# A graph message sum in blocks of 512 edges with one plain mask, made earlier and kept as bytes

## The reference, cut to what matters

```python
y = linear(layernorm(x)) * node_attr              # per node: 64 scalars y0, 64 vectors y1 of 3
w = silu(edge_scalars @ fc_w1) @ fc_w2            # per edge: 4 x 64 weights w0..w3
g0, g1 = y0[src], y1[src]                         # per edge, gathered
a = edge_attr[:, 1:4]                             # per edge: one vector of 3
scalars = [w0 * g0,  w2 * (g1 . a)]               # . is the sum over the 3 components
vectors = [w1 * g1,  (w3 * g0) * a]
agg = segment_sum([scalars, vectors], dst)        # per node: 8 x 64 numbers
```

## Time and profile before

| | us |
|---|---|
| median of 3 runs | 1990.52 (1987.57 to 1991.15) |
| the profiled execution | 1992.24 |
| its span, first instruction to last | 1990.5 |
| mean granted TensorE clock over the span | 0.938 of 2.4 GHz |
| busy: TensorE, VectorE, ScalarE, GpSimd | 1761.1, 1125.7, 1021.4, 1109.6 |

### The profile page before, as it was taken

How to read it: one execution, slowest core, us unless ns; L and a number is a source line. 1 busy time by engine, 2 the same in 40 slices (tenths; PEclk the granted TensorE clock), 3 DMA queues, 4 the chain that set the end, 5 groups by cost and what they waited for, 6 DMA issues and landing times. The chain is left out here.

```text
span 1990.5 us, 38467 instructions
## 1 busy us (share of the span) xinstructions
PE 1761.1 (88%) x9911; PEld 1434.7 (72%) x9911; DVE 1125.7 (57%) x2792; ACT 1021.4 (51%) x3052; POOL 1109.6 (56%) x1499
## 2 busy tenths in 40 slices
PE   2799999999899839999755999999999999995999
PEld 1466666666566729999634899888999887774887
DVE  6644333333411665544494999999999973233122
ACT  5455545555443612322246777777777745552221
POOL 6788888888600014555347888888888830000343
PEclk7899999999999559999977999999999999996999
DMA  8767777778640246667456777777777761564553
GB/s 235 221 214 248 246 238 242 242 238 266 210 153 0 65 103 213 208 212 217 148 126 204 210 218 215 215 214 218 216 213 218 209 172 52 172 188 116 177 176 120
DMA packets 229316, 376.43 MB, mean 189 GB/s; under 512 B 66200, under 2 KB 114427, under 8 KB 229117
## 3 DMA queue, kind: packets, MB, share of 16 engines
q1 hardware_dynamic: 174908, 222.13, 36.8%
q0 software_dynamic: 52224, 150.15, 25.2%
q10 hardware_dynamic: 1984, 1.79, 0.3%
HBM read 275.38 MB, written 99.57 MB: 188 GB/s over the span
## 5 line engine op out<-in xcount | busy, mean ns | idle before, releaser
L1963 POOL DMA_INDIRECT msg_got<-y_dram,block_src x416 | 417.9, 1004 | 101.7 <-issue 93.2
L441 POOL DMA_INDIRECT ffn_w<-xn_dram,block_src x384 | 364.4, 949 | 96.0 <-issue 87.5
L1984 ACT ACTIVATE msg_scaled<-msg_plain,msg_w 128x125 f32<-128x125 f32 x1044 | 312.0, 386 | 95.2 <-DVE msg_plain L2016 95.2
L556 PEld LDWEIGHTS sum_ps_bank<-ffn_w,sum_onehot 128*125 128x125 f32 x928 | 171.6, 193 | 191.1 <-issue 175.4
L556 PE MATMUL sum_ps_bank<-ffn_w,sum_onehot 128*125 x928 | 254.3, 399 | 50.0 <-DVE sum_onehot L898 26.1
L886 DVE TENSOR_TENSOR agg<-sum_ps_bank,agg 125x256 f32 x232 | 98.6, 425 | 282.9 <-PE sum_ps_bank L556 278.4
L655 ACT ACTIVATE sum_space<-sum_ps_bank,sum_rec 128x128 f32<-128x128 f32 x416 | 130.1, 364 | 202.1 <-PE sum_ps_bank L543 200.4
L543 PE MATMUL sum_ps_bank<-sum_fc,sum_space 128*128 128x512 f32 x416 | 211.5, 593 | 1.3 <-ACT sum_space L644 1.3
L2005 PEld LDWEIGHTS msg_ps_z<-msg_prod,msg_scaled 128*125 128x125 f32 x1416 | 174.5, 189 | 6.8
L2005 PE MATMUL msg_ps_z<-msg_prod,msg_scaled 128*125 128x128 f32 x1416 | 175.2, 274 | 0.0
L2045 DVE TENSOR_TENSOR agg<-msg_ps_z,agg 125x512 f32 x232 | 159.8, 689 | 22.0 <-DVE agg L2045 1.8
(11 more groups left out here) (346 smaller groups left out, 3252.5 us busy)
## 6 DMA issues: line engine op xcount, KB each, us to landing
edge_w<-sum_space SPq DMA_DIRECT2D x52, 1040.0 KB, 5.2
msg_w<-edge_w SPq DMA_DIRECT2D x174, 260.0 KB
ffn_run_w<-in_L_ffn_w SPq DMA_DIRECT2D x64, 512.0 KB
x_sb<-edge_w SPq DMA_DIRECT2D x58, 260.0 KB
ffn_rows<-agg SPq DMA_DIRECT2D x25, 448.0 KB
ffn_w<-in_L_ffn_w SPq DMA_DIRECT2D x16, 512.0 KB, 8.7
wd<-in_L_ffn_Wd SPq DMA_DIRECT2D x8, 1024.0 KB, 8.9
msg_got<-y_dram,block_src POOLq DMA_INDIRECT x416, 3.7
```

The source lines that it names most:

```text
L441: pool.indirect_dma_start(got[:, (b + 1) % RING, u, :], None, k.x if b < RAW else k.xn_dram, bass.IndirectOffsetOnAxis(ap=k.block_src[:, b ...
L556: last = pe.matmul(ps_sum[n % ZB][0:P, :], onehot[n % OB][:, u, :], got[:, ds(need % RING, 1), u, :].rearrange("p o d -> p (o d)"), start= ...
L1963: pool.indirect_dma_start(got[:, (b + 1) % RING, u, :, :].rearrange("p k v -> p (k v)"), None, k.y_dram, bass.IndirectOffsetOnAxis(ap=k.bl ...
L1984: last = act.activation(scaled[s % MB][:, x, c, :], plain[s % MB][:, c, :], ACT.Copy, scale=w[s % RS][:, c, D + x:D + x + 1])
```

## The change

The message stage goes over blocks of 512 edges instead of 256: NB4 = 104 blocks, NP4 = NB4 + T - 1 = 128 pairs, one step each, with four half blocks that all belong to the same pair.
- The three scaled masks are gone. One plain mask per half block sums all eight groups of 64 in a single product of 512 columns. What the scaled masks did is done on the values: VectorE forms g1 times a for the three components (`along`), adds them up, and multiplies by w2; ScalarE multiplies w3 * g0 (kept in a ninth slot of `prod`) by each component of a, twelve copies of 64 elements.
- The plain mask isn't compared in this stage. During the neighbour sum VectorE writes the masks of all 128 pairs as bytes, one instruction of 500 elements each (`mask_bytes`), spread over pairs 24 to 177. SyncE stores them to DRAM, four pairs at a time (256 KB). In the message stage SyncE loads them and ScalarE turns a pair's 500 bytes into floats.
- The tables for 512-edge pairs (`pair4_need`, `pair4_tile`, `pair4_dst`, `block4_done`) are made at the start of the neighbour sum, on VectorE and TensorE, ahead of the statistics of the gathered blocks. ScalarE's two copies of the edge attributes come after the third and fourth normalised group instead of the fourth and fifth.
- GpSimd's gathers stay 416 of the same size; its ring is 16 blocks of 512, and it looks for free room once in 16 blocks of 256, against a pair number that it loads from `block4_done`.

The diff, cut to its core:

```diff
@@ sum_neighbours
+    def bytes_due(n):
+        return min(NP4, max(0, (n - 24) * 5 // 6 + 1))
+    def bytes_from(j):
+        return j * 128 // 100
@@ SyncE
             for g in range(NW):
+                for j in range(NBY):
+                    if bytes_from(j) == g:
+                        sp.wait_ge(bytes_made, BY * (j + 1))
+                        sp.dma_start(k.bytes[j, :, :], held[j % HELD]).then_inc(bytes_stored[j % HELD], 16)
                 sp.wait_ge(w_kept, QB * (g + 1))
...
@@ TensorE
+            pe.wait_ge(four_ready, 5)
+            for h in range(2):
+                pe.matmul(ps_four[:, h:h + 1], ranks..., minus[:, h:h + 1], start=True, stop=(h == 0))
...
+            pe.wait_ge(past_made, 4)
+            pe.wait_ge(chosen_made, 4)
+            for h, (at, n) in enumerate(HALVES):
+                pe.matmul(ps_rows4[0:1, 0:NP4], even[0:n, :], past4[0:n, h, :], start=(h == 0), stop=(h == 1))
...
+            pe.wait_ge(shifted, 4)
+            pe.wait_ge(chosen_made, 6)
+            for c in range(CH):
+                for h, (at, n) in enumerate(HALVES):
+                    last = pe.matmul(ps_field4[:, c, :], dst_fb[h][0:n, :, c % KC], chosen_half[c // KC][0:n, h, :],
+                                     start=(h == 0), stop=(h == 1))
@@ ScalarE
-                if g == 3:
-                    act.wait_ge(tables_made, 1)
+                if g == 2:
+                    act.wait_ge(tables_made, 4)
@@ VectorE, between scales(4) and gathered_statistics(0)
+            dve.tensor_copy(ranks, k.tri[:, 0:128:2]...).then_inc(four_ready, 1)
+            dve.tensor_tensor(twins, ...)
...
+            dve.wait_ge(starts_ready, 2)
+            chain(dve.tensor_scalar(first4[:, :], ps_four[:, 0:2], -1.0, None, ALU.mult))
...
+            dve.wait_ge(rows_ready, 2)
+            chain(dve.tensor_tensor(tile4_row[0:1, :], ps_rows4[0:1, 128:128 + NP4], k.iota[0:1, 0:NP4], ALU.add))
...
+            dve.wait_ge(field_ready, 2)
+            dve.scalar_tensor_tensor(k.pair4_dst[:, :, :].rearrange("p n c -> p c n"), ...)
+            dve.wait_ge(tables_made, 4)
             gathered_statistics(0)
@@ VectorE, loop over the pairs
+            def mask_bytes(j):
+                if j % BY == 0 and j >= HELD * BY:
+                    dve.wait_ge(bytes_stored[j // BY % HELD], 16 * (j // (HELD * BY)))
+                dve.tensor_tensor(held[...], ps_lanes[:, :].unsqueeze(1).to_broadcast([128, CH, P]),
+                                  k.pair4_dst[:, j, :].unsqueeze(2).to_broadcast([128, CH, P]), ALU.is_equal).then_inc(bytes_made, 1)
                 if n >= 1:
                     add_sum(n - 1)
+                for j in range(bytes_due(n - 1), bytes_due(n)):
+                    mask_bytes(j)
@@ sum_messages, GpSimd
-                if b > AHEAD:
-                    pool.wait_ge(made, (b - AHEAD + 1) // 2)
+                if b >= 2 * RING4 and b % (2 * HOLD4) == 0:
+                    last = b // 2 - HOLD4 - 1
+                    done = pool.value_load(k.block4_done[0:1, last:last + 1], min_val=1, max_val=NP4)
+                    pool.wait_ge(made, done)
+                    pass_on(pool, freed)
@@ ScalarE
+            def mask(n):
...
+                act.activation(plain[n % MB]..., held[n // BY % YB][:, n % BY, :], ACT.Copy).then_inc(masked, 1)
+            def split(n):
+                act.wait_ge(opened, n + 1)
                 for c in range(CH):
                     for x in range(3):
-                        last = act.activation(scaled[s % MB][:, x, c, :], plain[s % MB][:, c, :], ACT.Copy, scale=...)
+                        last = act.activation(p[:, c, 5 + x, :], p[:, c, 8, :], ACT.Copy, scale=w[n % RS][:, c, D + x:D + x + 1])
@@ TensorE
+                for c in range(CH):
+                    last = pe.matmul(ps_z[n % ZB][0:P, :, :], plain[n % MB][:, c, :], prod[n % XB][:, c, 0:8, :],
+                                     start=(c == 0), stop=(c == CH - 1))
@@ VectorE
+            def open_products(n, need):
+                dve.tensor_tensor(p[:, :, 0:9:8, :], v[:, :, 0:4:3, :], y[:, :, 0:1, :].to_broadcast([128, CH, 2, MUL]), ALU.mult)
+                dve.tensor_tensor(t[:, :, :, :], y[:, :, 1:4, :], w[...][:, :, D:D + 3]..., ALU.mult).then_inc(along_made, 1)
+            def close_products(n, v, y):
+                dve.tensor_tensor(t[:, :, 0, :], t[:, :, 0, :], t[:, :, 1, :], ALU.add).then_inc(along_made, 1)
+                dve.tensor_tensor(p[:, :, 1:4, :], v[:, :, 1:2, :].to_broadcast([128, CH, 3, MUL]), y[:, :, 1:4, :], ALU.mult)
+                dve.wait_ge(along_made, 3 * n + 2)
+                dve.tensor_tensor(t[:, :, 0, :], t[:, :, 0, :], t[:, :, 2, :], ALU.add).then_inc(along_made, 1)
+                dve.wait_ge(along_made, 3 * n + 3)
+                dve.tensor_tensor(p[:, :, 4, :], v[:, :, 2, :], t[:, :, 0, :], ALU.mult).then_inc(made, 1)
```

289 lines of the change are left out of this document (172 added, 117 removed).

## The result

The changed kernel took 2046.81 us in the median (2043.9 to 2057.02), the kernel before 1990.0 beside it: ratio 1.0296, 95% interval 1.0257 to 1.0335. I had put 2003.5 and the range at 1990 to 2040: the sign was right, the size far too small.

What follows compares the result with a forecast made beforehand. GpSimd's gathers (544 us) were taken to bound the message stage, VectorE (531) close behind. Adding 12 us at the neighbour sum's start and 1 at the message stage gave 2005 profiled, 2003.5 as a median; range 1990 to 2040.

Steps and rivals of the forecast that it cites:

- What bounds the stage: Message stage before the change: GpSimd sets the pace with 544 us, VectorE stands close behind with 531.
- The long gathers: Message stage: gathers held up by VectorE products, assumed to cost the present 24 us after the change too.
- my upper bound: Message stage: every gather ending in a product waits to its end, mean 0.23 us, 95 us in all, GpSimd 615.
- Rival C: Message stage: products hold up GpSimd in earnest, +26 to +70 us, 2028 to 2070, mean gather over 1.06; chance 0.20.
- both halves: Message stage: two-SBUF-input VectorE instructions contend with GpSimd (towards 615 us); descriptor writing is not held up (towards 520).
- Start, +12 us (9 to 15): Start of the neighbour sum: new table work on VectorE and TensorE, without cover, delays it 12 us, bounds 9 and 15.
- Rival E: Neighbour sum's start: delay made good by quick pair sums, GpSimd's second wait ending 9 us sooner; 1985.5 us, chance 0.10.
- Masks and stores in the middle, nothing: Middle of the neighbour sum: 128 byte masks, 75 us of VectorE, hidden; 32 stores cost nothing.
- VectorE 4.20 us a pair: Message stage: VectorE's operations per pair of 512 edges sum to 4.20 us, x128 = 538 us, no gain against 531.
- Registers of GpSimd, 5 us: Message stage: GpSimd loads a number into a register eleven times, 0.5 us each assumed, 5 us.
- D, the clock: Message stage: TensorE, less busy, loses its full clock; +43 us at half the stage, about 2045 us; chance 0.05.
- B, gathers not held up: Message stage: GpSimd needs 520 + 5 us, VectorE's 4.20 us sets the pace; 1994.5 us (1990 to 1998), chance 0.18.

Runs made afterwards that it cites:

- thin: VectorE's message-stage products and sums cut to an eighth of their width: 1979.72 us in the changed kernel; the products likewise in the kernel before, 1972.55 us.
- the split kernel: The changed kernel with its opening, edge-vector and three-component products cut into operations of 256 elements each: 2047.06 us, ratio 1.0281.

## Why the prediction was wrong

- **What bounds the stage** (GpSimd, VectorE close behind): right, and more so after. 521 us is the 520 of my sum.
- **The long gathers, "I take the present 24 us"**: this is the step that failed, 24 in the sum against 80.9. Its reason was that the total of such time was small "although half of the stage is products". The total told of that kernel's moments only. There 224 gathers started inside a product, nearly as many as the 249 now, but late in a short one: they waited 0.10 us in the mean. Four reorderings of that kernel cost 17 to 33 us more in waits. The 95 us of my upper bound (each gather waits for the rest of a product) were nearer, though too small for what they were meant to bound: by my own step times the mean rest is 0.26 us and not 0.23, so 110 us. The 249 gathers waited 0.32 us in the mean. Rival C described what happened: mean gather 1.145, over its 1.06. Its chance of 0.20 was too small, and my range took in only half of it. The mechanism was half right: the products do it, but at a gather's start.
- **The rule of the Trainium skill** (SBUF — State Buffer, Who interferes with whom), of which I gave both halves: the first would have put my sum at 2003.5 + 95 - 24 = 2074, the second at 1994.5. The time lies between; the rows go with the first at a gather's start.
- **Start, +12 us (9 to 15)**: the tables took VectorE from 39.4 to 50.1, 10.7 us; the first pair sum came 10.8 later (58.51 against 47.75), block 32 9.7 later, the neighbour sum's last gather 9.6 later. The time for it is +6, not +12 or +10. That the first gather of the message stage came 7.6 us later in the mean of the ten kernels with the new neighbour sum (1080.6) than in the ten with the old (1073.0) says nearly the same. Where the other 3 us are won between 545 and 1070 us I have not found. Rival E, a delay made good by pair sums in quick succession, was wrong: from the first pair sum to block 32 it is 46.7 us against 47.7.
- **Masks and stores in the middle, nothing**: right. Block 32 to last gather 440.0 us against 440.0, VectorE busy 61 of 100 us.
- **VectorE 4.20 us a pair**: 4.17 from 1307.02 to 1311.19. **TensorE 3.44**: 3.67 for eight records, hidden. **ScalarE 3.5**: 2.98 + 0.60 = 3.58, hidden. **Registers of GpSimd, 5 us**: 0.6 at most (521.7 against 521.1). **End of the stage, 12 us behind the last gather**: 12.5. **D, the clock**: wrong, 0.99 from 1200 to 1400 us; that its 2045 is the single number nearest to the measured time is chance. **B, gathers not held up**: wrong, though its 520 us were reached once the products were thin.

## What to carry to other kernels

Where GpSimd's gathers set the pace, ask of each VectorE operation beside them whether it reads two SBUF operands, and at what moment gathers start; the sum of waits now is a mark of the present order and does not carry over to another one. As a rough upper estimate take the number of gathers times the share of time inside such operations times half the longest operation, and keep it in the range. Here that is 416 x 3.36 / 4.20 x 0.435 = 145 us against 80.9; it doesn't cover the long waits below. Longer, fewer operations make each wait longer; shorter ones cost VectorE time (4.55 us a step in place of 4.17), and an operation with a PSUM operand doesn't hold a gather up.

## What I had not expected of the hardware

- The wait is at the start of a gather: with 2048-element products (2.28 us) nearly every gather took 1.90 us and both engines ran at one period of 2.20 us. A gather that came first held a product up by 0.03 to 0.07 us only.
- `tensor_scalar` with one SBUF operand (768 elements in 0.59 us) holds up gathers (1.18 us) and a memset of GpSimd (0.44 in place of 0.14 us). The Trainium skill (SBUF — State Buffer, Who interferes with whom) says that `tensor_scalar` can enter modes that use two ports and contend with GpSimd; these rows agree.
- A gather can wait up to 1.8 us through several products up to the next operation with a PSUM operand; with a satisfied semaphore between the products none did. Why these 66 gathers and not others is open: in the split kernel 29 gathers, too, came 0.06 to 0.10 us before a product was through with another behind it and no semaphore between them, and waited for that one only.
- Register loads ahead of an operation cost 1.2 us a step on VectorE once its queue had to wait for semaphores just before them, and next to nothing without those semaphores (0.8 us in 120 additions). That the queue had run in advance there is my reading; no row shows the queue's lead.
- Open is what sets the phase between the two engines. A replay with row durations and the rule gave 10 to 70 us of waits for orders that measured 22 to 90, and it did not rank them.
